# A state-space layer with a mixture of experts: the memset in front of each scan moved from DVE to POOL, and the out-projection eviction cut in halves

## What is computed

```python
x = silu(dwconv(x)); z = silu(dwconv(z))            # 1024 channels each
dtr, Bm, Cm = split(x_proj(x), [64, 16, 16])
delta = softplus(dt_proj(dtr) + b)
dA = exp(delta[:, :, None] * A)                     # 16 states a channel
h  = dA * h + (delta * x)[:, :, None] * B_t         # scan over time
y  = sum_n(h * C_t) + D * x
s  = out_proj(concat(y, z))
```

## Time and profile before

| what | us |
|---|---|
| median of 2 runs | 4497.34 (4496.97 to 4497.7) |
| the profiled execution, its time | 4454.06 |
| its span, slowest core (core 6) | 4452.5 |
| spans of the 8 cores | 4415.4 to 4452.5 |
| PE busy | 2560.4 (58%) |
| DVE busy | 2274.8 (51%) |
| ACT busy | 2023.3 (45%) |
| POOL busy | 264.2 (6%) |
| memset of line 848 on DVE, 512 times | 31.2 |
| fixt, 480 times / dBx fix, 480 times | 67.7 / 82.6 |
| scans, 512 times | 1201.6 |
| eviction of line 477, 128x512, 64 times, median of one | 0.597 |

### The profile page before, as it was taken

The page is one execution under the profiler, slowest core; times in us unless marked ns, Lnnn a source line. Parts: engine busy times, 40 slices in busy tenths (PEclk is TensorE's granted clock), DMA queues, the critical chain, the costliest instruction groups (busy, mean ns, idle before and its releaser), DMA issues.

```text
span 4452.5 us, 70266 instructions; the slowest of 8 cores (4415.4 to 4452.5 us)
## 1 busy us (share of the span) xinstructions
PE 2560.4 (58%) x17792; PEld 1921.6 (43%) x17792; DVE 2274.8 (51%) x2949; ACT 2023.3 (45%) x4169; POOL 264.2 (6%) x386
## 2 busy tenths in 40 slices
PE   1204656575665656566665656656575665657565
PEld 1103544353444435354443534444353444435344
DVE  0204454564846456384545638454554846456484
ACT  1303363544636354463635446363544636354462
POOL 0100010101001010100101010010101001010100
PEclk9556877787877888778787878778787777878678
DMA  7796433343443334343333434333443433344343
GB/s 106 114 110 151 127 127 114 133 128 114 130 128 128 116 130 125 123 129 120 121 118 131 129 113 134 119 124 119 131 131 113 130 126 126 116 131 129 112 133 102
DMA packets 329922, 549.76 MB, mean 123 GB/s; under 512 B 20457, under 2 KB 170090, under 8 KB 324530
## 3 DMA queue, kind: packets, MB, share of 16 engines
q1 hardware_dynamic: 319554, 473.49, 34.2%
q0 software_dynamic: 9968, 71.77, 8.5%
HBM read 557.31 MB, written 46.47 MB: 136 GB/s over the span
## 4 chain that ended last, share of the span: by engine, by line
PE 35%; ACT 21%; DMA 17%; issue 12%; DVE 6%; another core or an unknown queue 6%; POOL 2%; SPq 0%; DVEq 0%; ACTq 0%; POOLq 0%
PE P L259 33%; ACT dA L823 8%; DMA sb_out<-blob_out 5%; DMA sb_w<-blob_w 4%; ACT scrb L939 3%; ACT L939 2%; DMA x_f<-x_t 2%; DMA sb_cd<-blob_cd 2%; DMA sb_in<-blob_in 2%; POOL delta L703 2%; PE P L532 1%; DMA bc_dram<-bcB 1%; ACT stage L686 1%; DVE dBx L816 1%
## 5 line engine op out<-in xcount | busy, mean ns | idle before, releaser
L852 DVE TENSOR_TENSOR_SCAN h_b<-dA,carry,dBx 128x1024 bf16<-128x1024 f32 x480 | 1128.3, 2351 | 82.9 <-DVE dA L848 82.5
L823 ACT ACTIVATE dA<-delta,A_neg 128x256 f32<-128x256 f32 x2048 | 858.7, 496 | 621.6 <-DVE fixt L835 588.1
L259 PE MATMUL P<-xn_b,sb_w 128*128 128x256 bf16 x4096 | 639.8, 326 | 578.9 <-ACT scrb L939 443.4
L259 PEld LDWEIGHTS P<-xn_b,sb_w 128*128 128x128 bf16 x4096 | 460.1, 115 | 754.3 <-issue 637.0
L259 PE MATMUL P<-scrb,sb_w 128*128 128x256 bf16 x4096 | 488.7, 278 | 57.3 <-DMA sb_w<-blob_w 56.9
L259 PEld LDWEIGHTS P<-scrb,sb_w 128*128 128x128 bf16 x4096 | 405.5, 100 | 122.4 <-issue 67.7
L259 PE MATMUL P<-xn_b,sb_in 128*128 128x256 bf16 (+1 forms) x2176 | 315.1, 311 | 204.2 <-DMA sb_in<-blob_in 134.2
L816 DVE TENSOR_TENSOR dBx<-u_b,Bb 128x4096 bf16<-128x4096 bf16 x128 | 293.9, 2296 | 246.6 <-DMA Bb<-bc_dram 206.7
L939 ACT ACTIVATE scrb<-P,b1c 128x256 bf16<-128x256 f32 x512 | 242.4, 473 | 306.6 <-PE P L259 269.1
L949 DVE TENSOR_TENSOR scrb<-scrb,ge_all 128x1024 bf16<-128x1024 bf16 x128 | 88.4, 691 | 537.7 <-ACT scrb L939 301.5
L259 PEld LDWEIGHTS P<-xn_b,sb_in 128*128 128x128 bf16 x2176 | 229.6, 113 | 295.3 <-issue 239.6
(11 more groups left out here) (115 smaller groups left out, 2520.0 us busy)
## 6 DMA issues: line engine op xcount, KB each, us to landing
sb_w<-blob_w SPq DMA_DIRECT2D x512, 512.0 KB, 4.3
sb_in<-blob_in SPq DMA_DIRECT2D x256, 256.0 KB, 3.4
sb_out<-blob_out SPq DMA_DIRECT2D x128, 512.0 KB, 4.3
sb_cd<-blob_cd SPq DMA_DIRECT2D x128, 256.0 KB, 3.8
Bb<-bc_dram POOLq DMA_DIRECT2D x16, 1024.0 KB, 5.3
Cb<-bc_dram POOLq DMA_DIRECT2D x16, 1024.0 KB, 7.2
blob_w<-w_w POOLq DMA_DIRECT2D x2, 8192.0 KB, 123.6
out<-stage SPq DMA_DIRECT2D x32, 512.0 KB, 3.1
```

The costliest lines, as they stand in the source:

```text
L259: return eng.matmul(out_ap, lhsT, rhs, start=first, stop=last, skip_group_check=True)
L823: return eng.activation(sb["dA"][:, slot * 256:(slot + 1) * 256], sb["delta"][:, g * 256:(g + 1) * 256], AF.Exp, scale=sb["A_neg"][:, g * ...
L852: return eng.tensor_tensor_scan(sb["h_b"][:, q0 * 256:(q0 + 4) * 256], apv(sb["dA"], s0 * 256, [[1, 1024]]), apv(sb["dBx"], dko + q0 * 256 ...
```

## The change

Two edits. First, in `out_proj_a_evac` the eviction of a PSUM bank by one 128x512 copy becomes two copies of 128x256, each writing the name of its own eighth of s_f; the order of the banks (P7, P6, P4, P5) stays. Second, the memset of the scan's batch is added to POOL's list instead of DVE's, with the same names, at the same place of the list.

```diff
         def out_proj_a_evac(i, js):
-            done = set()
             for j in js:
-                q = j // 2
-                if q in done:
-                    continue
-                done.add(q)
-                bank = "P%d" % (4 + q)
-                def fe(eng, q=q, bank=bank):
-                    return eng.activation(sb["s_f"][:, q * 512:(q + 1) * 512],
-                                          ps[bank][:, :], AF.Copy)
-                S.add("act", fe, reads=(bank,),
-                      writes=("s:%d" % (2 * q), "s:%d" % (2 * q + 1)),
-                      tag="ope%d.%d" % (i, 2 * q))
+                bank = "P%d" % (4 + j // 2)
+                half = (j % 2) * 256
+                def fe(eng, j=j, bank=bank, half=half):
+                    return eng.activation(sb["s_f"][:, j * 256:(j + 1) * 256],
+                                          ps[bank][:, half:half + 256], AF.Copy)
+                S.add("act", fe, reads=(bank,), writes=("s:%d" % j,), tag="ope%d.%d" % (i, j))
...
                     def fz(eng, s0=s0):
                         return eng.memset(apv(sb["dA"], (s0 + 1) * 256, [[256, 3], [1, 1]]), 0.0)
-                    S.add("dve", fz, reads=bkeys, writes=bkeys, tag="sfz%d.%d.%d" % (i, g, q0))
+                    S.add("gp", fz, reads=bkeys, writes=bkeys, tag="sfz%d.%d.%d" % (i, g, q0))
```

## The result

| | before | after |
|---|---|---|
| median of runs | 4455.16 us (10 runs, 4447.17 to 4497.7) | 4517.52 us (11 runs, 4504.15 to 4571.59) |
| ratio after/before, 95% interval | | 1.0152 [1.0107, 1.0197] |
| profiled execution, its span | 4454.06, 4452.5 | 4516.05, 4514.5 |

A forecast was written before the change was run, and what follows sets the result against it. Scans of groups 0 to 5, alternating with ACT's exponentials, were taken as the steady path, DMA as the start's bound. Terms 45.5 + 17 + 0 + 0 = 62.5 us on 4497.3 gave 4560 us, range 4525 to 4604.

The forecast's parts named there:

- Group 0: Each later chunk's first memset queues on POOL behind ge_dram and ge_all, delaying the first scan: +45.5 us, 3.0 a chunk.
- Chunk 0: Eight memsets stand ahead of the five weight casts on POOL, so casts go out later: +17 us (12 to 21.5).
- the gap: Empty DMA stretch ahead of the later casts, where the last two sb_cd loads now travel: 4.5 us off.
- A steady batch: POOL's memset branch, 0.52 us, stays just under the dBx branch, so the 2.87 us step stays: 0.
- The prediction's +0.10: Upper bound a batch, if POOL's memset had to stand behind the dBx fix: scan start at 0.70, not 0.60.
- The eviction: Eight out_proj copies instead of four: +1.3 us a chunk on ACT, hidden while it idles before the convolution ends: 0.
- the last one of the sum: Adding the 62.5 us, taken from the profiled execution, to the median of the runs, 4497.3, giving 4560 us.
- Rival 1: The hand-over through POOL is the longer branch of a steady batch: +0.10 a batch, 4594 us; chance 0.20.
- Rival 2: Later casts in chunk 0 cost little, so only the 45.5 us stays: 4543 us; chance 0.12.
- Rival 3: Without the memset the scan closes up to the dBx fix: −0.225 a batch, 4484 us; chance 0.04.

The follow-up runs named there:

- experiment 3: Changed kernel with the five weight casts issued right behind ge_all of chunk 0, ahead of the memsets: 4506.95 us, ratio to before 1.0111 [1.0057, 1.0164].
- experiment 4: Changed kernel with the gate broadcast (ge_dram, ge_all) issued behind the memsets of group 0: 4476.37 us, ratio to before 1.0044 [1.0012, 1.0077].
- experiment 6: Changed kernel with each batch's memset issued twice on POOL, the second waiting for the first: 4543.69 us, ratio to before 1.0221 [1.0193, 1.0249].
- experiment 7: Changed kernel with the memset replaced by an in-place POOL multiplication by zero, which reads SBUF: one execution, 4540.15 us.
- experiment 2: Kernel before with only the out_proj eviction halved into eight 256-wide copies, memset still on DVE: 4453.29 us, ratio 0.9998 [0.9963, 1.0033].
- experiment 5: Changed kernel with the casts ahead of the memsets and, from chunk 1 on, the gate broadcast behind group 0: 4455.75 us, ratio to before 1.0 [0.9972, 1.0028].

## Why the prediction was right, and where it was wrong

**The mechanism and the rows came as forecast, the difference nearly.** That 62.5 meets the 62 between the medians to the microsecond is luck: the ratio gives 68 [48, 88], the eight-core means 67.5, and both terms of the sum were a little low.

- *Group 0*: forecast 45.5 us, 3.0 a chunk. The eight-core means give 3.08 a chunk; experiment 3, with this cost alone, gave +50 [25, 73]. The first scan came 4.18 us behind ge_dram in the rows shown, and over the 15 chunks 3.6 on average on core 1 and 3.5 on all cores (forecast 3.7).
- *Chunk 0*: forecast 17 us (12 to 21.5). Measured +20.4 at the next chunk's start, +20 [5, 34] in experiment 4 (whose own chunk 0 cost 14.4 in its profiled execution, with casts 6 us earlier than in after). The casts went out at 177.65 (forecast 177.5); the SP load at 383.86 (forecast 383), and of the 21.7 us by which the casts were later, 18.0 reached it. What came off is the gap: the last sb_cd loads, for which PE had waited 47.08 and 37.74 us, now landed ahead of the casts and held PE for 1.09.
- *A steady batch*: forecast 0. The step is 2.87 before and after. The POOL branch was priced at 0.52 from the start of fixt to the earliest scan; its memset starts 0.26 after fixt and takes 0.10, and POOL to DVE takes 0.11 (experiment 6): 0.47. The margin was 0.13, not 0.08. The second wait of the scan has no price that a step shows, and the memset starts and ends inside the dBx fix. The prediction's +0.10 was for a POOL operation that stands behind that fix, as the delta addition had stood behind a product; in experiment 7 even an operation that reads isn't stretched by the short fix (0.23 us with and without it), though it is by a scan or a product.
- *The eviction*: forecast 0; experiment 2 says 0.9998 [0.9963, 1.0033], so within 17 us. The right result from a wrong price: eight copies take 0.25 us more a chunk, not 1.3, since these copies of 256 columns take 0.29 us each (37.0/128) where the exponentials of the same width take 0.43 (1.70/4).

**The step that failed is the last one of the sum**: "microseconds added to one are added to the other: 4497.3 + 62.5 = 4560". They were added to the median of two runs that stood 43 us above the profiled execution from which each term came. Of the ten runs of before, three stand at 4497 (both of those two among them) and seven between 4447 and 4462. Of the 42.5 us of error the base is 42.2 (4497.34 − 4455.16). With the same sum from the profiled execution: 4454.06 + 62.5 = 4516.6, against 4516.05 for that of after and a median of 4517.52. The text saw the 43 us, and neither asked which of the two a third run would resemble nor let the range reach down by it. A range from both bases would have begun near 4482.

**The rivals.** Rival 1 (+0.10 a batch) didn't come: POOL releases 22 scans, not 338, and experiment 6 shows how it would have shown itself. Rival 2 (chunk 0 costs little) fell with experiment 4. Rival 3 (−0.225 a batch) fell by the step: with the memset gone the scan starts 0.18 after the end of the dBx fix, where it started 0.17 after the end of the memset. The rule cited there from the Trainium skill ("VectorE: DVE Perf Modes", section "Rules for kernel authors"), fewer operations, would have given −39 us, by the prediction's estimate from 0.115 us a batch; experiment 5, which has DVE's 512 instructions fewer and the queue put right, gives 1.0 [0.9972, 1.0028]. The removed instruction lay in the shadow of its neighbour.

**Small and unforeseen.** In chunk 0, where there is no dBx fix, scans follow each other in 2.53 us (158.17 to 160.70 in after) where it was 2.46: the idle before them is 0.24 to 0.25. The scan's own list of waits is now ACT, POOL and its predecessor; that this is the cause is not shown. It concerns 32 batches, so 2 us at most.

## What to carry to other kernels

An operation moved to an engine with time to spare moves into a queue: read what stands ahead of it there, above all an issue that waits for a DMA, and what then stands behind it, above all an issue that starts a long transfer. Here an operation of 0.1 us cost over 60 us by its place alone, and with two places of the order put right no cost could be measured. And a difference read from one execution is added to the time of that execution; when the runs at hand disagree with it, both bases belong in the range.

## What the runs showed of the hardware that I had not expected

- The row length of a big cast decides how long small loads wait beside it, not only its bytes (the short rows are also taken in another order, which no run here tells apart). A 256 KB load that lands in 3.8 us (median over the program) held PE for 47.08 and 37.74 us beside the big casts of before, 32.75 and 28.19 beside sixteen casts in whole rows, and 14.90 and 0.97 beside the same sixteen in short rows. At 99% DMA share this moved the start of the experts from 337 to 206 us.
- The rate of the stretch rose as well, from 111 to 140 GB/s at the same share of 0.98 to 0.99. What of this is the shape of the rows and what the mix with the experts' loads, no run here tells apart.
- GpSimd's memset of 384 elements takes 0.10 us in the middle of a DVE scan or product; a multiplication of the same elements, 0.23 us alone, takes until that DVE operation ends (0.61 and 1.87 us). Beside the dBx fix of 0.17 us it takes 0.23.
